# Seeding the key and value banks with their biases from ScalarE in place of a bias matmul, in a linear-attention and FP4 feed-forward layer

## What is computed

```
q = elu(x @ Wq + bq) + 1
k = elu(x @ Wk + bk) + 1;  v = x @ Wv + bv
k = k / sqrt(sum over a head of k*k + 1e-6)
attn = (q k^T) v, no softmax, 16 heads of 16
x1 = LN(x + LN(x + attn @ Wo + bo) * gamma + beta)
out = LN(x1 + fp4_linear(silu(gate) * up))
```

## Time and profile before

| what | value |
|---|---|
| median of 3 runs | 699.68 us (699.58 to 700.99) |
| the profiled execution | 699.75 us, of which its span 698.0 us |
| PE busy | 682.8 us, 98% of the span |
| POOL, DVE, ACT busy | 607.8, 584.3, 488.9 us |
| granted clock of TensorE | 0.998 |

### The profile page before, as it was taken

The page is one execution under the profiler, slowest core; times in us unless marked ns, Lnnn a source line. Parts: engine busy times, 40 slices in busy tenths (PEclk is TensorE's granted clock), DMA queues, the critical chain, the costliest instruction groups (busy, mean ns, idle before and its releaser), DMA issues.

```text
span 698.0 us, 14240 instructions
## 1 busy us (share of the span) xinstructions
PE 682.8 (98%) x4370; PEld 602.7 (86%) x4370; DVE 584.3 (84%) x1441; ACT 488.9 (70%) x954; POOL 607.8 (87%) x947
## 2 busy tenths in 40 slices
PE   8999999999999999999999999999999999999995
PEld 6888888888877899999999999999999999999995
DVE  6678778876778899889989989998998998998774
ACT  4677777766777676776677677677677767767664
POOL 3988898988888999898999989899899988989766
PEclk9999999999999999999999999999999999999999
DMA  8544443344301111121221122122111211100001
GB/s 278 179 137 136 137 140 119 133 157 152 108 31 36 56 47 46 46 83 70 77 74 50 44 79 87 51 76 77 46 64 59 77 45 48 60 17 16 21 28 45
DMA packets 23135, 56.36 MB, mean 81 GB/s; under 512 B 2642, under 2 KB 5908, under 8 KB 23060
## 3 DMA queue, kind: packets, MB, share of 16 engines
q1 hardware_dynamic: 22640, 55.32, 23.2%
q10 hardware_dynamic: 420, 0.13, 0.1%
HBM read 30.22 MB, written 25.17 MB: 79 GB/s over the span
## 4 chain that ended last, share of the span: by engine, by line
PE 91%; DVE 3%; issue 2%; POOL 2%; ACT 1%; DMA 1%; POOLq 0%; SPq 0%; DVEq 0%
PE banks L407 23%; PE banks L408 22%; PE banks L409 22%; PE banks L553 8%; PE banks L524 7%; PE banks L445 2%; PE banks L418 2%; PE banks L567 1%; PE banks L566 1%; PE banks L431 1%; PE banks L476 1%; DMA resid<-in_L_attn_Wk_dram 1%; PE banks L484 1%; POOL arena L1166 1%; DVE arena L838 0%
## 5 line engine op out<-in xcount | busy, mean ns | idle before, releaser
L407 PE MATMUL banks<-wgu_hi,actT_lo 128*128 128x512 f32 (+1 forms) x384 | 149.8, 390 | 3.0 <-DVE actT_lo L958 1.5
L408 PE MATMUL banks<-wgu_lo,actT_hi 128*128 128x512 f32 (+1 forms) x384 | 144.0, 375 | 0.0
L409 PE MATMUL banks<-wgu_hi,actT_hi 128*128 128x512 f32 (+1 forms) x384 | 143.3, 373 | 0.0
L725 ACT ACTIVATE arena<-banks 128x512 f32<-128x512 f32 x64 | 38.3, 599 | 111.9 <-PE banks L409 111.8
L1166 POOL TENSOR_TENSOR arena<-arena 128x960 f32<-128x960 f16 (+2 forms) x68 | 115.1, 1693 | 0.0
L1142 POOL TENSOR_TENSOR arena<-arena 128x704 f32<-128x704 f32 x64 | 91.7, 1433 | 20.7 <-DVE arena L945 18.7
L407 PE MATMUL banks<-wd_hi,actT_lo 128*128 128x256 f32 x320 | 100.1, 313 | 0.0
L958 DVE TENSOR_TENSOR actT_lo<-banks,actT_hi 128x512 fp32r<-128x512 f32 (+1 forms) x132 | 85.4, 673 | 16.3 <-ACT actT_hi L711 15.6
L409 PE MATMUL banks<-wd_hi,actT_hi 128*128 128x256 f32 x320 | 90.2, 282 | 0.0
L408 PE MATMUL banks<-wd_lo,actT_hi 128*128 128x256 f32 x320 | 90.2, 282 | 0.0
L407 PEld LDWEIGHTS banks<-wgu_hi,actT_lo 128*128 128x128 f32 x384 | 72.5, 189 | 12.6 <-DVE actT_lo L958 2.3
(11 more groups left out here) (126 smaller groups left out, 1915.5 us busy)
## 6 DMA issues: line engine op xcount, KB each, us to landing
xs<-x_plus_scratch SPq DMA_DIRECT2D x32, 512.0 KB, 3.3
x_plus_scratch<-xs SPq DMA_DIRECT2D x24, 512.0 KB, 2.9
arena<-in_L_attn_x_dram SPq DMA_DIRECT2D x32, 256.0 KB, 3.5
out_dram<-arena SPq DMA_DIRECT2D x32, 256.0 KB, 2.1
x_plus_scratch<-arena SPq DMA_DIRECT2D x4, 512.0 KB, 2.9
x_plus_scratch<-resid SPq DMA_DIRECT2D x4, 512.0 KB, 2.7
resid<-in_L_attn_x_dram SPq DMA_DIRECT2D x4, 256.0 KB, 3.7
resid<-in_L_ffn_w_down_dram SPq DMA_DIRECT2D x1, 704.0 KB, 7.9
```

Source lines behind the costliest of these rows:

```text
L407: nc.tensor.matmul(dst, sl, mh, start=(k == 0), stop=False, skip_group_check=shared)
L408: nc.tensor.matmul(dst, sh, ml, start=False, stop=False, skip_group_check=shared)
L409: last = nc.tensor.matmul(dst, sh, mh, start=False, stop=(ended and k == n - 1), skip_group_check=shared)
```

## The change

For pairs 2 to 23 (`filled`) PE issues no bias matmul. Instead ACT writes both biases, in one activation of 128x1024, from SBUF into the two banks of the pair, and the first matmul of `kv_project` adds to what is there. ACT does this for pair p+1 at step p, behind the query maps and ahead of the exp of pair p; once, ahead of the first, it adds 1 to bk. It waits until keys and values of the pair that had the banks before have been read, and `kv_project` waits for it. `v_bias` of these pairs becomes a plain copy. `mask_heads` moves from step 6, 10, ... (ahead of the query features) to step 5, 9, ... (behind `v_bias`, ahead of the sums of squares). `kv_accumulate` is no longer early in steps with `chunk_at(p - 3)`, which are 5, 7, 9, ..., 21, 22 and 23. SP loads bk to all partitions once more, behind beta; bo gets a buffer of its own.

```
+        bo_b = sb("bo_b", [P, D])
-        bv_b, bo_b = words(9587, D), words(9843, D)
+        bkv = words(9587, 2 * D)
+        bv_b = bkv[:, D:2 * D]
+        def filled(p):
+            return 2 <= p < MERGE
+            sp.dma_start(bkv[:, 0:D], bk.partition_broadcast(P)).then_inc(bk_in, 16)
             load_x(2)
...
+                if filled(p):
+                    pe.wait_ge(kv_bias, p - 1)
                 for jj in range(2):
...
+                    last = split_product(..., KT, begun=filled(p), ended=filled(p), shared=True)
+                    if not filled(p):
+                        last = nc.tensor.matmul(ps[:, bank, 0:D], rows[:, D:], rows[:, 0:D], start=False, stop=True,
+                                                skip_group_check=True)
...
-                early = 4 <= p < MERGE and (p - 2) % PPB > 0
+                early = 4 <= p < MERGE and (p - 2) % PPB > 0 and chunk_at(p - 3) is None
...
+            def kv_biases(p):
+                if p == 2:
+                    act.wait_ge(bk_in, 16)
+                    act.wait_ge(bv_in, 16)
+                    nc.scalar.activation(bkv[:, 0:D], bkv[:, 0:D], ACT.Copy, bias=1.0).then_inc(bk_one, 1)
+                    act.wait_ge(bk_one, 1)
+                act.wait_ge(k_feat, p - 1)
+                act.wait_ge(v_s, p - 1)
+                b = kv_banks(p)
+                nc.scalar.activation(ps[:, b:b + 2, :], bkv[:, :].unsqueeze(1).broadcast_to([P, 2, 2 * D]),
+                                     ACT.Copy).then_inc(kv_bias, 1)
...
                 if pair(p - 2):
                     q_maps(p - 2)
+                if filled(p + 1):
+                    kv_biases(p + 1)
...
+                if filled(p):
+                    nc.vector.tensor_copy(vb[:, p % 3, :, :], ps[:, b:b + 2, D:2 * D]).then_inc(v_s, 1)
...
-                if p == 6:
-                    dve.wait_ge(consts_set, 4)
-                if p >= 6 and (p - 6) % PPB == 0 and (p - 6) // PPB < B - 1:
-                    mask_heads((p - 6) // PPB)
                 if pair(p - 2):
                     q_features(p - 2)
...
                     k_features(p)
                     v_bias(p)
+                if p == 5:
+                    dve.wait_ge(consts_set, 4)
+                if p >= 5 and (p - 5) % PPB == 0 and (p - 5) // PPB < B - 1:
+                    mask_heads((p - 5) // PPB)
                 if pair(p):
                     k_sums(p)
```

More of the change, by code:

```diff
@@ L177, in build @@
         G_BANK, U_BANK, GU_BANK, T_BANK, AT_BANK, DN_BANK = 6, 7, 0, 4, 2, (3, 1)
-        wk_in, wv_in, wq_in, wffn_in, rows_in, bv_in, bq_in, xb_in, late_in = (
-            sem(n) for n in ("wk_in", "wv_in", "wq_in", "wffn_in", "rows_in", "bv_in", "bq_in", "xb_in", "late_in"))
+        wk_in, wv_in, wq_in, wffn_in, rows_in, bv_in, bq_in, bk_in, xb_in, late_in = (
+            sem(n) for n in ("wk_in", "wv_in", "wq_in", "wffn_in", "rows_in", "bv_in", "bq_in", "bk_in", "xb_in", "late_in"))
         consts_set, small_set, cols_set, mask_s = sem("consts_set"), sem("small_set"), sem("cols_set"), sem("mask")
@@ L190, in build @@
         xT_ps, xT_hi_s, xT_lo_s = sem("xT_ps"), sem("xT_hi_done"), sem("xT_lo_done")
+        bk_one, kv_bias = sem("bk_one"), sem("kv_bias")
         kv_ps, k_exp, k_feat, v_s, k_sq, k_ssq, k_se, k_log, k_seed = (
@@ L402, in _, with split_product @@
         def _(pe):
-            def split_product(dst, stat, mov, n, ended=True, shared=False):
+            def split_product(dst, stat, mov, n, begun=False, ended=True, shared=False):
                 for k in range(n):
                     (sh, sl), (mh, ml) = stat(k), mov(k)
-                    nc.tensor.matmul(dst, sl, mh, start=(k == 0), stop=False, skip_group_check=shared)
+                    nc.tensor.matmul(dst, sl, mh, start=(not begun and k == 0), stop=False, skip_group_check=shared)
                     nc.tensor.matmul(dst, sh, ml, start=False, stop=False, skip_group_check=shared)
@@ L428, in kv_project @@
                     c = slice((p % PPB) * 2 * P + jj * P, (p % PPB) * 2 * P + (jj + 1) * P)
[L429 to L432, removed]
+                    last = split_product(ps[:, bank, :], lambda k: (xT_hi[:, k, c], xT_lo[:, k, c]),
+                                         lambda k: (wkv_hi[:, k, :], wkv_lo[:, k, :]), KT, begun=filled(p), ended=filled(p),
+                                         shared=True)
+                    if not filled(p):
+                        last = nc.tensor.matmul(ps[:, bank, 0:D], rows[:, D:], rows[:, 0:D], start=False, stop=True,
+                                                skip_group_check=True)
                 last.then_inc(kv_ps, 1)
@@ L843, in v_bias @@
                 b = kv_banks(p)
-                nc.vector.tensor_tensor(vb[:, p % 3, :, :], ps[:, b:b + 2, D:2 * D],
-                                        bv_b[:, :].unsqueeze(1).broadcast_to([P, 2, D]), ALU.add).then_inc(v_s, 1)
+                if filled(p):
+                    nc.vector.tensor_copy(vb[:, p % 3, :, :], ps[:, b:b + 2, D:2 * D]).then_inc(v_s, 1)
+                else:
+                    nc.vector.tensor_tensor(vb[:, p % 3, :, :], ps[:, b:b + 2, D:2 * D],
+                                            bv_b[:, :].unsqueeze(1).broadcast_to([P, 2, D]), ALU.add).then_inc(v_s, 1)
             def k_sums(p):
```

## The result

The changed kernel takes 704.12 us (median of 7 runs, 702.67 to 705.3), the kernel before 700.7 us in 7 runs beside it (699.58 to 701.39). The ratio is 1.0045, 95% interval 1.0034 to 1.0057: slower by some 3.15 us. Forecast was +3.4.

The account below looks back on a forecast made before the run. PE bounds the kernel before; ACT replaces it in the first stage. ACT's 1.4 + 19.95 - 18.6 + 1.0 = 3.75 us reaches PE as 3.4: 699.75 + 3.4 = 703.15 us, range 697.5 to 705.5 (8 in 10).

Parts of the forecast that it names:

- What bounds the kernel, and which idle time is spare: First stage: PE bounds; of ACT's idle 36 us only 13.2 and 3.3 us of waiting for PE are spare.
- The price of a write: Each 128x1024 activation for pairs 2 to 23 costs ACT's list 0.93 to 0.97 us, taken as 0.95.
- lower bound: Duration of one 1024-column ACT write: 591 ns for 512 columns plus 512 x 0.84 ns, 1.02 us.
- Step 1: ACT's copy adding 1 to bk, 0.42 us, and one write, 0.95, together +1.4 us ahead of an exp.
- Steps 2 to 22: ACT's list: 21 writes at 0.95, +19.95 us; spare time takes off 18.6, masked heads add 1.0.
- spare time: ACT up to exp 23: PE waits 13.2 + 3.3 and returning overlap 2.5, less small losses, together 18.6 us.
- The hand-over to PE: At step 23 weights_turn waits for query features; of ACT's 3.75 us lag, kv_project(24) starts 3.4 us later.
- rival 1: PE keeps the bound: 694.6 us; partial forms, including shift taken back between 190 and 235 us, 695 to 698; chance 0.17.
- The sum: Whole kernel: 699.75 us, of which 1.75 lie around the span, plus 3.4 gives 703.15 us.
- At nothing: v_bias as a copy, the second bk load and waits for freed banks were each taken to cost nothing.
- What goes from PE: 22 pairs x 2 bias matmuls x 0.12 us, 5.2 us off PE; moving kv_accumulate takes nothing off.

Follow-up runs that it names:

- e2: Kernel after, ACT's write kept and PE's 44 bias matmuls back, DVE adding bv again: 704.08 us, ratio 1.0036 to the kernel before.
- e3: Kernel after with ACT's write cut to one bank, 512 columns instead of 1024, second tile without bias: 695.67 us, ratio 0.992 to before.
- e4: Kernel after with the masked heads back at their old place, a step later and ahead of the query features: 703.78 us, ratio 1.0035 to before.
- e7: Kernel after with kv_accumulate early in steps 5, 7, 9, ..., 23 as before: 703.95 us, ratio 1.0042 to the kernel before.
- e5: Kernel after with ACT's write only for ten pairs (p % 4 < 2), bias matmuls for the others: 697.9 us, ratio 0.9957 to before.
- e6: Kernel after with ACT's write only for fifteen pairs (p > 3 and p % 4 < 3): 698.92 us, ratio 0.9976 to the kernel before.
- e8: Kernel before with only masked heads a step sooner and kv_accumulate late; bias matmuls stay, no ACT write: 700.77 us, ratio 0.9992 to before.
- e1: Kernel after with neither bias matmuls nor ACT's write for pairs 2 to 23: 694.24 us, ratio 0.9906 to the kernel before.

## Why the prediction was right

- *What bounds the kernel, and which idle time is spare.* Right. Of ACT's 36 us without work only the part that ended with PE was there to be filled; the 16.7 us behind DVE came back as 16.6. e2 and e3 show the two halves of it: PE's work is free, ACT's length is not.
- *The price of a write.* 1.01 us of duration (mean 1014 ns), just under the lower bound of 1.02. The next instruction starts 0.06 to 0.07 us before its end, not 0.09, so the net price is 0.95, the value taken. The Trainium skill, ScalarE: Activation LUTs, section Step-by-step: what each stage is for, says that an ACTIVATE whose destination is PSUM is faster than one to SBUF. The trace agrees: 584 ns for 512 columns to PSUM (e3) against 632 for a square of 512 from and to SBUF, and 1014 against the 1060 worked out from 16-bit SBUF rows. These 46 to 48 ns are 1 us over 22 writes; the sum had them already in its 0.95, and the sign does not hang on them.
- *Step 1.* Exp 0 to exp 1 grew from 3.46 to 4.87 us: +1.41, forecast +1.4.
- *Steps 2 to 22.* Exp 1 to exp 23 grew from 131.14 to 132.58 us: +1.44, forecast 19.95 - 18.6 + 1.0 = +2.35. The term that was mis-sized is the spare time: with the masks at 0.8 (four steps of 0.20, forecast 1.0) it was 19.95 + 0.8 - 1.44 = 19.3 us, not 18.6. Two of its parts can be worked out. ACT's busy time in this stretch rose from 94.97 to 111.94 us, by 17.0 where 21 writes at 0.95 are 19.95; so 3.0 us of overlap came back, not 2.5. And the wait for the sums of squares grew from 1.7 us to 2.2 without the new place of the masks (e4), so 0.5 returned, not 0.7.
- *The hand-over to PE.* Right in kind and in size, wrong in its place: the wait that counted stood a step sooner than forecast, 0.72 us before `kv_out` of step 22, which also needs query features, and the sum had no term for it; at step 23 the two paths came level. That 0.14 lies near 0.35 is partly luck. Exp 23 came 4.30 us later, `kv_project(24)` at 152.57 instead of 148.41, 4.16 later: the step took back 0.14 us, not 0.35. From there on exp 25 to exp 31 keep a shift of 4.1 to 4.2 us, and the whole span has 4.3: nothing is taken back between 190 and 235 us, one of the partial forms of rival 1.
- *The sum.* 1.41 + 1.44 - 0.14 = +2.7 us in the profiled execution without its late start, +3.15 (2.4 to 4.0) in the runs, +3.4 forecast. Some 0.3 us more lie outside the span, which the prediction held at 1.75: time less span is 2.00 to 2.07 us in the runs of the kernel after, and as much in e2, e3, e4 and e7, but 1.68 to 1.78 in those of before, e5, e6 and e8, and 1.74 to 1.89 in e1. No run shows why. With it the account comes to +3.0.
- *At nothing.* `v_bias` as a copy takes 683 ns (22 of them), the add 0.69 us: nothing gained or lost. The bk load delayed nobody that the trace shows: neither PE nor PEld waits for a transfer between 10 and 18 us. No write waits for its banks.
- *What goes from PE.* 5.2 us was a little low; e1 shows 5.9, and the order alone 0.6 (e8). It played no part while ACT was the bound.

What stays open: the 0.3 us outside the span, why the clock fell behind the stall of e4 and at some starts and not at others, and whether the write would cost less elsewhere in ACT's list, which no run tried.

## What to carry to other kernels

Before work moves from the bound engine to one with free time, split the free time by what ends it: a wait for the engine that is to be relieved is spare. A wait between two instructions that stand side by side in the list, of which the second needs what a third engine makes of the first, is not spare: nothing stands between them that could fill it. Here 36 us of idle ACT held 19 of spare, and 21 were asked of them. When the sum doesn't fit, move a part: ten pairs gave 3 us, all twenty-two cost 3. And work at a fixed place of each step changes the waits around it: fifteen writes cost 0.9 us more than fifteen times the price of one.

## What the runs showed of the hardware

TensorE waited 1.70 us for the masks in e4 and then ran at about half speed: granted clock 0.54 from 142.9 to 146.5 us, matmuls of 512 columns 0.43 us apart instead of 0.23. At the start, around the waits for the first x, matmuls of 512 columns stood 0.43 us apart for 2 to 3.5 us in the profiled executions of after, e3, e6 and e8 and for some 5 us in that of e7, and 0.23 in those of before, e1, e2, e4 and e5. The length of the wait alone doesn't decide: e5 waited 1.55 us for x of pair 1 and kept its speed, after waited 1.67 and lost it. The granted clock of 8.4 to 12.4 us was 0.57 in after and e8, but 1.00 in e3, e6 and e7, so that the record of the clock doesn't account for every slow stretch. Exp 0 came 1.3 to 1.5 us later than before in the first four and 2.5 in e7, which was not foreseen; a change of this size needs several runs to be told from it.

An activation from SBUF into two banks of PSUM at once took 1.01 us for 1024 columns, and one into a single bank 0.58 us for 512 (e3), with TensorE busy for 127.7 of the 132.6 us from exp 1 to exp 23.
